# Half of the residual row carried by each of a token's two expert results, in a top-2 mixture-of-experts block

## The chip, the cores and the metric

The kernel runs on one core of a Trainium2 chip. The metric is the device time of one execution in microseconds (us), median of several runs. Five engines work beside each other and meet only through semaphores: TensorE (PE), VectorE (DVE), ScalarE (ACT), GpSimd (POOL) and SyncE (SP), which here only issues DMAs.

## The reference, cut to what matters

One sequence of 2048 tokens of 128 numbers in float32 goes through one layer: gated linear attention, a layer norm, a feed-forward stage of 8 experts of which each token uses its best 2, and a second layer norm.

```python
x = _layernorm(x + attn(x))                    # no scale and no shift in the norm
# expert stage
scores = x @ Wr + br
weights = softmax(scores of the best 2 of 8)   # 0 elsewhere
for i in range(E):
    h = relu(x @ W1[i] + b1[i])
    out += (h @ W2[i] + b2[i]) * weights[i]
return _layernorm(x + out)
```

The row `x` added in the last line is the residual row that the change is about.

## The kernel before, in words

Tokens are held in T = 16 tiles of 128: token 128 t + p lies in partition p of tile t. The program has four stages.

1. Projections (first 59 us). `x_sb` [128, 16, 128] is loaded and transposed by PE; q, k, v, the gates and the decay factors are made by PE, ACT and DVE. Meanwhile SP issues the DMAs that fill the DRAM buffer `expert_rows` with padding rows (L389), then those of the second expert weights and biases (L391, L393). GpSimd makes constants, scales the first group of keys (`scale_k(0)`), and then waits for all padding rows (`pool.wait_ge(s_pad, 16 * E)`, L493), since it is to scatter real rows over them.
2. Attention and routing (59 to 145.6 us), a software pipeline over the 16 tiles. DVE's `residual(t)` (L886) adds `x_sb` to the attention output in PSUM, `mean_var` and ACT's `inverse_std` (L643, L647) give the norm's factors, and `normalize` (L925) writes the normalized row to `xr[:, t, 0, 0:D]`; ACT copies it to `xr[:, t, 1, 0:D]`, and its transpose to `x1T` (L633) for the router matmul. GpSimd scatters each token's row twice (once for each expert, with the weight in column D and the number of the result row in column D + 1) into `expert_rows` by indirect DMA (L489).
3. Experts (145.6 to 247.5 us). 39 slots of 128 rows, each of one expert. For each slot SP gathers the rows to `xg` (L407) and 2 of 3 slots' first weights; PE transposes the rows (L1321), ACT copies the transpose to `xgT` (L688), PE makes the hidden layer (L1333) and the output (L1346), ACT and DVE apply bias and relu (L698, L1066), DVE adds the bias `b2` (L1074) and multiplies by the token's weight (`weighted`, L1079, into `yw`). GpSimd takes the result row numbers (L529, `dest`) and scatters the 128 rows of `yw` to `expert_results` by indirect DMA (L533). Every third slot's first weights are loaded from GpSimd's queue (L373).
4. The last stage (247.5 to 266.0 us). A token's two results lie next to each other in `expert_results`. SP loads them in 8 groups of FT = 2 tiles (L417, `ysum`). For each group GpSimd adds the first result to the residual row in `xr` (L546), DVE adds the second result (L1100), takes `bn_stats` and `bn_aggr` of both tiles (L1103, L1106), ACT makes 1/sqrt(var + eps) with a Ln and an Exp (L714, L716), DVE makes the shift -mean/std (`shift`, L1095, one group behind), ACT applies scale and shift to each tile (L721), and SP stores the group (L421).

Each engine's order is its program order as written; nothing is scheduled otherwise. The functions that the diff touches:

Of the kernel before, what the change touches and what calls it, by code (L numbers as in the profile page):

```python
# [24 lines left out]
def build(nc, x, Wq, Wk, Wv, Wg, Wgk1, Wgk2, bgk2, Wo, g_norm, Wr, br, W1, b1, W2, b2, out):  # L25
# [23 lines left out]
    out_tok = out.rearrange("a (t p) d -> p (a t) d", p=P)  # L49
    rows = nc.dram_tensor("expert_rows", [E * CAP, ROW], F32, kind="Internal").ap()  # L50
    results = nc.dram_tensor("expert_results", [TOP * N, D], F32, kind="Internal").ap()

    with ExitStack() as ctx:
        def sb(name, shape, dt=F32):
            return ctx.enter_context(nc.sbuf_tensor(name, shape, dt))
# [126 lines left out]
        fshift = sb("fshift", [P, T])  # L182
# [21 lines left out]
        s_w2 = sem("w2_loaded")  # L204
        s_seed = sem("constants_zeroed")
# [82 lines left out]
        s_acc0 = sem("first_result_added")  # L288
        s_acc = sem("second_result_added")
# [4 lines left out]
        s_fshift = sem("final_shift")  # L294
# [83 lines left out]
        def _(sp):  # L378
# [37 lines left out]
            for g in range(T // FT):  # L416
                sp.dma_start(ysum[:, g * FT:(g + 1) * FT, :],  # L417
                             results[g * FT * P * TOP:(g + 1) * FT * P * TOP, :].rearrange("(t p k) d -> p t (k d)", p=P, k=TOP)).then_inc(s_ysum[g], 16)
            for g in range(T // FT):
                sp.wait_ge(s_result, (g + 1) * FT)  # L420
                sp.dma_start(out_tok[:, g * FT:(g + 1) * FT, :], result[:, g * FT:(g + 1) * FT, :]).then_inc(s_stored, 16)  # L421
# [3 lines left out]
        def _(pool):  # L425
# [38 lines left out]
            count_up(xr[:, :, :, ROW - 1], [[TOP * P, T], [1, TOP]], 0, TOP)  # L464
            def scale_k(g):
                c = slice(g * GROUP, (g + 1) * GROUP)
                t = slice(g * TG, (g + 1) * TG)
                pool.wait_ge(s_eq, 2 * (g + 1))
                pool.tensor_tensor(km[:, c], kT[:, c], ek[:, g % 2, :], ALU.mult).then_inc(s_km, 1)  # L469
                pool.wait_ge(s_km, g + 1)  # L470
                pool.tensor_tensor(tiles(kc[:, c]), tiles(km[:, c]), wide(er[:, t], P), ALU.mult).then_inc(s_kc, 1)
# [71 lines left out]
            for g in range(T // FT):  # L543
                t = slice(g * FT, (g + 1) * FT)
                pool.wait_ge(s_ysum[g], 16)
                pool.tensor_tensor(acc[:, t, :], ysum[:, t, 0:D], xr[:, t, 0, 0:D], ALU.add).then_inc(s_acc0, 1)  # L546

        @block.scalar
        def _(act):
# [80 lines left out]
            def copy_x1T(t):  # L630
                if t >= 2:
                    act.wait_ge(s_dve_bank, t - 2 + AGE_ROUTE)
                act.activation(x1T[:, t % 2, :], bank[6][:, P:2 * P], ACT.Copy).then_inc(s_x1T, 1)  # L633
# [5 lines left out]
            def inverse_std(t):  # L639
# [3 lines left out]
                act.activation(lstd[:, b, :], mv[:, b, 1:2], ACT.Ln, bias=eps_sb[:, :]).then_inc(s_lstd, 1)  # L643
# [39 lines left out]
            def copy_rows(i):  # L683
                h = i % 3
                act.wait_ge(s_gt, i + 1)
                if i >= 3:
                    act.wait_ge(s_hb, i - 2)
                act.activation(xgT[:, h, :], bank[7][:, 0:P], ACT.Copy).then_inc(s_gT, 1)  # L688
# [21 lines left out]
            for g in range(T // FT + 1):  # L710
                if g < T // FT:
                    t = slice(g * FT, (g + 1) * FT)
                    act.wait_ge(s_fmv, (g + 1) * FT)
                    act.activation(flog[:, t], fmv[:, t, 1], ACT.Ln, bias=eps_sb[:, :]).then_inc(s_flog, 1)  # L714
                    act.wait_ge(s_flog, g + 1)
                    act.activation(frstd[:, t], flog[:, t], ACT.Exp, scale=-0.5).then_inc(s_frs, 1)  # L716
                if g:
                    act.wait_ge(s_frs, g)
                    act.wait_ge(s_fshift, g)
                    for n in range((g - 1) * FT, g * FT):  # L720
                        act.activation(result[:, n, :], acc[:, n, :], ACT.Identity, bias=fshift[:, n:n + 1],  # L721
                                       scale=frstd[:, n:n + 1]).then_inc(s_result, 1)

        @block.vector
        def _(dve):
# [94 lines left out]
            dve.tensor_scalar(wo_sb[:, :, :], wo_in[:, :, :], gnorm_sb[:, 0:1], None, ALU.mult).then_inc(s_wo2, 1)  # L820
# [64 lines left out]
            def residual(t):  # L885
                dve.tensor_tensor(res[:, t % 2, :], bank[7][:, 256:256 + D], x_sb[:, t, :], ALU.add).then_inc(s_res, 1)  # L886
# [182 lines left out]
            def weighted(i):  # L1069
# [9 lines left out]
                dve.tensor_scalar(yw[:, u, :], yb[:, h, :], xg[:, u, D:D + 1], None, ALU.mult).then_inc(s_yw, 1)  # L1079
# [11 lines left out]
            def shift(g):  # L1091

                t = slice(g * FT, (g + 1) * FT)
                dve.wait_ge(s_frs, g + 1)
                dve.scalar_tensor_tensor(fshift[:, t], fmv[:, t, 0], -1.0, frstd[:, t], ALU.mult, ALU.mult).then_inc(s_fshift, 1)  # L1095

            for g in range(T // FT):
                t = slice(g * FT, (g + 1) * FT)
                dve.wait_ge(s_acc0, g + 1)
                dve.tensor_tensor(acc[:, t, :], acc[:, t, :], ysum[:, t, D:2 * D], ALU.add).then_inc(s_acc, 1)  # L1100
                dve.wait_ge(s_acc, g + 1)
# [5 lines left out]
                if g:  # L1107
                    shift(g - 1)
            shift(T // FT - 1)
# [277 lines left out]
```

## Time and profile before

| | |
|---|---|
| median of 3 runs | 265.79 us (264.65, 265.79, 267.12) |
| span of the profiled execution | 266.0 us, 0.2 us above the median |
| busy: PE, DVE, POOL, ACT | 185.6, 159.6, 119.0, 110.9 us |
| stage borders used here | 59, 145.6, 247.5, 266.0 us |

The profiled execution is listed by its span alone, from the first to the last instruction; no other time of that execution is shown. Times in the profile are microseconds from the span's start. A timeline row holds the start, the duration, the engine, the line of the kernel, the operation with its output and inputs, and how many instructions are merged in it. "[4.01 <-DMA ...]" says how long the engine had sat idle before, and what ended that. SPq and POOLq are the queues that issue DMAs. Where a row merges several instructions, its duration is that of the whole run of them.

### The profile page before, as it was taken

What the parts mean: (1) busy time and instruction counts of PE and PEld (TensorE: products, weight loads), DVE (VectorE), ACT (ScalarE), POOL (GpSimd) and SP (SyncE); (2) the same over time, 40 slices, a digit from 0 to 9 for tenths busy, and PEclk for the clock granted to TensorE, in tenths of its full rate; (3) what the DMA queues carried; (4) which work ended last, traced back from release to release, by engine and by line L of the source; (5) the groups of instructions that cost most, each with busy time, mean ns of one, the idle gap of its engine ahead of it and who ended that gap; (6) DMA issues with size and microseconds to landing.
All of it is one profiled execution on the core that took longest, in us unless ns stands there. A gap on an engine that the chain in (4) does not pass through costs nothing.

```text
span 266.0 us, 5740 instructions
## 1 busy us (share of the span) xinstructions
PE 185.6 (70%) x1289; PEld 150.2 (56%) x1289; DVE 159.6 (60%) x593; ACT 110.9 (42%) x345; POOL 119.0 (45%) x188
## 2 busy tenths in 40 slices
PE   2999959205886898896652188999889998994000
PEld 1556427104654676664541178989889898893000
DVE  5399937005989988878676022555555556563293
ACT  1188764201645355454530022444434434440086
POOL 5000400014522746556576614566666666666270
PEclk9999995955999799999855557999999999999555
DMA  5999999998000010010011445466666575630563
GB/s 166 254 187 194 199 174 183 188 196 264 0 2 1 10 34 24 27 34 30 30 41 50 110 150 159 135 194 192 192 184 185 184 182 177 175 108 1 178 198 99
DMA packets 39553, 33.87 MB, mean 127 GB/s; under 512 B 3806, under 2 KB 33172, under 8 KB 39520
## 3 DMA queue, kind: packets, MB, share of 16 engines
q1 hardware_dynamic: 35264, 25.68, 45.5%
q0 software_dynamic: 3312, 7.64, 8.1%
q10 hardware_dynamic: 944, 0.17, 0.3%
q8 instruction: 12, 0.20, 0.3%
q14 instruction: 21, 0.17, 0.2%
HBM read 19.15 MB, written 14.79 MB: 128 GB/s over the span
## 4 chain that ended last, share of the span: by engine, by line
issue 49%; SPq 24%; POOL 12%; PE 4%; DVE 3%; DMA 3%; POOLq 2%; ACT 2%; DVEq 0%; ACTq 0%
SPq L389 15%; POOL expert_results L533 8%; SPq L393 4%; POOL dest L529 2%; PE psum L1333 2%; SPq L391 2%; ACT x_sb L721 1%; PE psum L1346 1%; POOLq L363 1%; DMA gate<-expert_results 1%; DVE fstats L1103 1%; DMA expert_results<-kT,dest 1%; DMA xg<-expert_rows 1%; SPq L380 1%; DVE xT L1100 1%
## 5 line engine op out<-in xcount | busy, mean ns | idle before, releaser
L533 POOL DMA_INDIRECT expert_results<-kT,dest x39 | 38.4, 985 | 36.3 <-issue 18.2
L1346 PE MATMUL psum<-w_sb,gT 128*128 x312 | 44.0, 286 | 0.5 <-issue 0.3
L1066 DVE TENSOR_SCALAR gT<-psum,b_sb 128x128 f32<-128x128 f32 x78 | 23.8, 347 | 32.3 <-PE psum L1333 19.1
L1346 PEld LDWEIGHTS psum<-w_sb,gT 128*128 128x128 f32 x312 | 39.4, 198 | 2.2 <-issue 1.3
L489 POOL DMA_INDIRECT expert_rows<-xr,slot x32 | 31.4, 980 | 13.1 <-issue 10.8
L698 ACT ACTIVATE gT<-psum,b_sb 128x128 f32<-128x128 f32 x78 | 24.4, 363 | 18.2 <-issue 15.5
L688 ACT ACTIVATE kT<-psum 128x128 f32<-128x128 f32 x39 | 10.8, 277 | 46.0 <-PE psum L1321 37.0
L469 POOL TENSOR_TENSOR km<-kT,ek 128x512 f32<-128x512 f32 x4 | 5.1, 1279 | 50.7 <-DMA expert_rows<-pad_row 25.9
L1333 PE MATMUL psum<-kT,km 128*128 128x128 f32 x168 | 24.2, 292 | 5.1 <-issue 5.1
L1333 PEld LDWEIGHTS psum<-kT,km 128*128 128x128 f32 x168 | 22.0, 205 | 6.1 <-issue 6.1
L479 POOL TENSOR_TENSOR rgate<-rrms,gate 128x256 f32<-128x256 f32 x16 | 12.0, 752 | 27.7 <-ACT rrms L625 26.7
L1235 PE MATMUL psum<-wo_sb,ogT 128*128 128x128 f32 x64 | 11.8, 316 | 15.5 <-DVE ogT L919 15.5
L1333 PE MATMUL psum<-kT,qm 128*128 128x128 f32 x144 | 20.2, 286 | 1.6 <-issue 1.6
L1074 DVE TENSOR_TENSOR kT<-psum,b_sb 128x128 f32<-128x128 f32 x39 | 11.4, 292 | 16.0 <-issue 9.6
L1235 PEld LDWEIGHTS psum<-wo_sb,ogT 128*128 128x128 f32 x64 | 11.0, 222 | 16.8 <-DVE ogT L919 14.5
L1333 PEld LDWEIGHTS psum<-kT,qm 128*128 128x128 f32 x144 | 18.3, 200 | 2.2 <-issue 2.2
L900 DVE SCALAR_TENSOR_TENSOR state<-state,tile_decay,psum 32x64 f32<-32x64 f32 x60 | 16.3, 272 | 2.3 <-PE psum L1230 0.7
L620 ACT ACTIVATE lrms<-psum,eps_sb 128x256 f32<-128x256 f32 x16 | 7.5, 471 | 23.6 <-PE psum L1226 17.8
L919 DVE TENSOR_TENSOR ogT<-psum,rgate 128x256 f32<-128x256 f32 x16 | 6.8, 423 | 15.8 <-POOL rgate L479 15.4
L1321 PE MATMUL psum<-ident,xg 128*128 128x128 f32 x39 | 11.3, 290 | 6.8 <-DMA xg<-expert_rows 6.8
L1221 PE MATMUL psum<-sq,block_ones 128*128 128x256 f32 x32 | 11.9, 455 | 3.5 <-ACT sq L651 2.8
L882 DVE COPY_PREDICATED aT<-keep,psum 128x512 f32<-128x512 int32 x16 | 11.6, 724 | 4.0 <-PE psum L1195 3.9
(169 smaller groups left out, 382.6 us busy)
## 6 DMA issues: line engine op xcount, KB each, us to landing
expert_rows<-pad_row SPq DMA_DIRECT2D x8, 1105.0 KB, 18.8
km<-in_L_ffn_W_dram SPq DMA_DIRECT2D x14, 256.0 KB
qm<-in_L_ffn_W_dram SPq DMA_DIRECT2D x12, 256.0 KB
xg<-expert_rows SPq DMA_DIRECT2D x39, 65.0 KB
gate<-expert_results SPq DMA_DIRECT2D x8, 256.0 KB, 4.6
km<-in_L_ffn_W_dram POOLq DMA_DIRECT2D x7, 256.0 KB
qm<-in_L_ffn_W_dram POOLq DMA_DIRECT2D x6, 256.0 KB
x_sb<-in_L_attn_x_dram SPq DMA_DIRECT2D x4, 256.0 KB, 4.3
```

Source lines behind the costliest of these rows:

```text
L389: sp.dma_start(rows[e * CAP:(e + 1) * CAP, :].rearrange("(n p) c -> p n c", p=P), pad_row[:, :].unsqueeze(1).to_broadcast([P, CAP // P, RO ...
L479: pool.tensor_tensor(rgate[:, t % 2, :, :], rrms[:, t % 2, :, :], gate[:, :, t * P:(t + 1) * P], ALU.mult).then_inc(s_rg, 1)
L489: pool.indirect_dma_start(out=rows[:, :], in_=xr[:, t, k, :], in_offset=None, out_offset=bass.IndirectOffsetOnAxis(ap=slot[:, t, k:k + 1], ...
L533: pool.indirect_dma_start(out=results[:, :], in_=yw[:, u, :], in_offset=None, bounds_check=TOP * N - 1, oob_is_err=False, out_offset=bass. ...
L698: act.activation(hT[:, h, n, :], bank[2 * (i % 2)][:, n * P:(n + 1) * P], ACT.Relu, bias=b1_sb[:, bass.ds(e * HC + n, 1)]).then_inc(s_hTa, 1)
L882: dve.copy_predicated(aT[:, t % 2, :, :], keep[:, :].unsqueeze(1).to_broadcast([P, HEADS, P]), psum[:, 0:HEADS, 0:P]).then_inc(s_aT, 1)
L900: ins = dve.scalar_tensor_tensor(state[r, t % 2, v], state[r, (t - 1) % 2, v], tile_decay[r, t:t + 1], bank[7][r, v], ALU.mult, ALU.add)
L1066: dve.tensor_scalar(hT[:, h, HC // 2 + n, :], bank[2 * (i % 2) + 1][:, n * P:(n + 1) * P], b1_sb[:, bass.ds(e * HC + HC // 2 + n, 1)], 0.0 ...
L1221: return mm(bank[6][:, 256:512], block_ones[:, :], sq[:, t % 2, :, :].rearrange("p c t -> p (c t)"), start=True, stop=True)
L1235: last = mm(bank[7][:, 256:256 + D], ogT[:, t % 2, c, :], wo_sb[:, c, :], start=(c == 0), stop=(c == DVC - 1))
L1333: last = mm(bank[2 * (i % 2) + half][:, k * P:(k + 1) * P], w1_buf[u][:, n * P:(n + 1) * P], xgT[:, h, :], start=True, stop=True)
L1346: last = mm(bank[4 + i % 2][:, 0:D], hT[:, h, n, :], w2_all[:, bass.ds(first + n * D, D)], start=(n == 0), stop=(n == HC - 1))
```

## The change: what it does

- GpSimd multiplies all of `x_sb` by 0.5 once, after the last transpose of it, and the projection `Wo` is multiplied by 0.5 besides its norm weight. So the sum of residual and attention is half of what it was; `inverse_std` multiplies the variance by 4, and the normalized row in `xr` comes out at half its value. The router's and the experts' inputs are doubled back in the copies that ACT makes anyway (`scale=2.0`).
- In the expert stage DVE's last step of a slot becomes `scalar_tensor_tensor`: bias output times weight, plus the gathered (half) row. A token's two results then sum to residual plus expert output.
- In the last stage partition p holds tokens 16 p to 16 p + 15, so a group of 2 tokens is one piece of 2 KB per partition in DRAM when loaded (before: 2 pieces of 1 KB) and 1 KB when stored (before: 2 of 512 B). The two results are added by DVE in the even groups and by GpSimd in the odd ones. GpSimd, no longer ACT, applies mean and 1/std, with `tensor_scalar` on each 128x128 tile; the shift step is gone.

```diff
-    out_tok = out.rearrange("a (t p) d -> p (a t) d", p=P)
+    out_rows = out.rearrange("a (p j) d -> p (a j) d", p=P)
+    results_tok = results.rearrange("(p j k) d -> p j (k d)", p=P, k=TOP)
@@ SP, last stage
-                sp.dma_start(ysum[:, g * FT:(g + 1) * FT, :],
-                             results[g * FT * P * TOP:(g + 1) * FT * P * TOP, :].rearrange("(t p k) d -> p t (k d)", p=P, k=TOP)).then_inc(s_ysum[g], 16)
+                sp.dma_start(ysum[:, g * FT:(g + 1) * FT, :], results_tok[:, g * FT:(g + 1) * FT, :]).then_inc(s_ysum[g], 16)
-                sp.dma_start(out_tok[:, g * FT:(g + 1) * FT, :], result[:, g * FT:(g + 1) * FT, :]).then_inc(s_stored, 16)
+                sp.dma_start(out_rows[:, g * FT:(g + 1) * FT, :], result[:, g * FT:(g + 1) * FT, :]).then_inc(s_stored, 16)
@@ GpSimd, before scale_k(0)
+            pool.wait_ge(s_job, at["xT", NG - 1] + 1)
+            pool.tensor_scalar(x_sb[:, :, :], x_sb[:, :, :], 0.5, None, ALU.mult).then_inc(s_xhalf, 1)
@@ GpSimd, last stage
             for g in range(T // FT):
-                t = slice(g * FT, (g + 1) * FT)
-                pool.wait_ge(s_ysum[g], 16)
-                pool.tensor_tensor(acc[:, t, :], ysum[:, t, 0:D], xr[:, t, 0, 0:D], ALU.add).then_inc(s_acc0, 1)
+                if g % 2 == 0:
+                    t = slice((g + 1) * FT, (g + 2) * FT)
+                    pool.wait_ge(s_ysum[g + 1], 16)
+                    pool.tensor_tensor(acc[:, t, :], ysum[:, t, 0:D], ysum[:, t, D:2 * D], ALU.add).then_inc(s_acc_odd, 1)
+                pool.wait_ge(s_frs, g + 1)
+                for n in range(g * FT, (g + 1) * FT):
+                    pool.tensor_scalar(result[:, n, :], acc[:, n, :], fmv[:, n, 0:1], frstd[:, n:n + 1],
+                                       ALU.subtract, ALU.mult).then_inc(s_result, 1)
@@ ACT
-                act.activation(x1T[:, t % 2, :], bank[6][:, P:2 * P], ACT.Copy).then_inc(s_x1T, 1)
+                act.activation(x1T[:, t % 2, :], bank[6][:, P:2 * P], ACT.Copy, scale=2.0).then_inc(s_x1T, 1)
-                act.activation(lstd[:, b, :], mv[:, b, 1:2], ACT.Ln, bias=eps_sb[:, :]).then_inc(s_lstd, 1)
+                act.activation(lstd[:, b, :], mv[:, b, 1:2], ACT.Ln, bias=eps_sb[:, :], scale=4.0).then_inc(s_lstd, 1)
-                act.activation(xgT[:, h, :], bank[7][:, 0:P], ACT.Copy).then_inc(s_gT, 1)
+                act.activation(xgT[:, h, :], bank[7][:, 0:P], ACT.Copy, scale=2.0).then_inc(s_gT, 1)
@@ ACT, last stage: Ln and Exp stay, the scaling goes
-                if g:
-                    act.wait_ge(s_frs, g)
-                    act.wait_ge(s_fshift, g)
-                    for n in range((g - 1) * FT, g * FT):
-                        act.activation(result[:, n, :], acc[:, n, :], ACT.Identity, bias=fshift[:, n:n + 1],
-                                       scale=frstd[:, n:n + 1]).then_inc(s_result, 1)
@@ DVE
-            dve.tensor_scalar(wo_sb[:, :, :], wo_in[:, :, :], gnorm_sb[:, 0:1], None, ALU.mult).then_inc(s_wo2, 1)
+            dve.tensor_scalar(wo_sb[:, :, :], wo_in[:, :, :], gnorm_sb[:, 0:1], 0.5, ALU.mult, ALU.mult).then_inc(s_wo2, 1)
             def residual(t):
+                if t == 0:
+                    dve.wait_ge(s_xhalf, 1)
-                dve.tensor_scalar(yw[:, u, :], yb[:, h, :], xg[:, u, D:D + 1], None, ALU.mult).then_inc(s_yw, 1)
+                dve.scalar_tensor_tensor(yw[:, u, :], yb[:, h, :], xg[:, u, D:D + 1], xg[:, u, 0:D],
+                                         ALU.mult, ALU.add).then_inc(s_yw, 1)
@@ DVE, last stage (the calls of shift(g) go too)
-                dve.wait_ge(s_acc0, g + 1)
-                dve.tensor_tensor(acc[:, t, :], acc[:, t, :], ysum[:, t, D:2 * D], ALU.add).then_inc(s_acc, 1)
-                dve.wait_ge(s_acc, g + 1)
+                if g % 2:
+                    dve.wait_ge(s_acc_odd, g // 2 + 1)
+                else:
+                    dve.wait_ge(s_ysum[g], 16)
+                    dve.tensor_tensor(acc[:, t, :], ysum[:, t, 0:D], ysum[:, t, D:2 * D], ALU.add).then_inc(s_acc, 1)
+                    dve.wait_ge(s_acc, g // 2 + 1)
```

## Rows read from the trace of the kernel before

**Rows 1.** The stretches of the four stages: busy time by engine, granted clock, DMA.

```profile
0.00:59.00 59.00, 39.99 (x159) 23.79 (x159) 32.69 (x77) 27.35 (x50) 6.34 (x27) 0.89 1.16 192
59.00:145.60 86.60, 62.24 (x467) 46.89 (x467) 68.77 (x312) 38.34 (x146) 47.45 (x56) 0.85 0.14 44
145.60:247.50 101.90, 83.36 (x663) 79.51 (x663) 47.90 (x156) 35.17 (x117) 58.62 (x97) 0.92 0.53 153
247.50:266.00 18.50, 0.00 (x0) 0.00 (x0) 10.29 (x48) 10.07 (x32) 6.57 (x8) 0.50 0.55 171
```

**Rows 2.** The chain that ended last: its shares of the span by line.

```profile
SPq L389 15%; POOL expert_results L533 8%; SPq L393 4%; POOL dest L529 2%; PE psum L1333 2%; SPq L391 2%; ACT x_sb L721 1%; PE psum L1346 1%; POOLq L363 1%; DMA gate<-expert_results 1%; DVE fstats L1103 1%; DMA expert_results<-kT,dest 1%; DMA xg<-expert_rows 1%; SPq L380 1%; DVE xT L1100 1%
```

**Rows 3.** Timeline around the padding wait, 48 to 62 us.

```profile
48.90 0.26 ACT L628 ACTIVATE kcT<-psum 128x128 f32<-128x128 f32 x1
...
59.01 1.26 POOL L469 TENSOR_TENSOR km<-kT,ek 128x512 f32<-128x512 f32 x1 [25.91 <-DMA expert_rows<-pad_row]
...
62.10 0.42 DVE L919 TENSOR_TENSOR ogT<-psum,rgate 128x256 f32<-128x256 f32 x1 [15.05 <-POOL rgate L479]
```

**Rows 4.** Timeline of the projections: PE's last transpose, then DVE.

```profile
12.03 0.60 PE L1126 MATMUL psum<-ident,x_sb 128*128 128x128 f32 x4
...
15.17 0.68 DVE L771 SCALAR_TENSOR_TENSOR gT<-km,qm 128x512 f32<-128x512 f32 x1
```

**Rows 5.** Timeline of the expert stage's end, 242 to 247 us.

```profile
242.80 0.29 DVE L1079 TENSOR_SCALAR kT<-kT,xg 128x128 f32<-128x128 f32 x1
243.32 0.98 POOL L533 DMA_INDIRECT expert_results<-kT,dest  x1 [0.78 <-DVE kT L1079]
...
245.27 0.97 POOL L533 DMA_INDIRECT expert_results<-kT,dest  x1 [0.78 <-POOL dest L529]
```

**Rows 6.** Timeline of the last stage: loads, the first group, ACT's final run.

```profile
247.48 4.16 SPq L417 DMA_DIRECT2D gate<-expert_results  x8
250.26 1.76 POOL L546 TENSOR_TENSOR xT<-gate,xr 128x256 f32<-128x256 f32 x2 [4.01 <-DMA gate<-expert_results]
...
251.47 0.49 DVE L1103 BATCH_NORM_STATS2 fstats<-xT 128x6 f32<-128x128 f32 x2
251.87 0.30 DVE L1106 BATCH_NORM_AGGREGATE fmv<-fstats 128x2 f32<-128x6 f32 x2
...
252.21 0.30 ACT L714 ACTIVATE flog<-fmv,eps_sb 128x2 f32<-128x2 f32 x1 [11.81 <-DVE fmv L1106]
...
252.54 0.20 ACT L716 ACTIVATE frstd<-flog 128x2 f32<-128x2 f32 x1
...
262.08 1.63 ACT L721 ACTIVATE x_sb<-xT,fshift,frstd 128x128 f32<-128x128 f32 x4
```

**Rows 7.** GpSimd's groups by shape: count, busy us, mean ns, idle before.

```profile
L529 POOL CAST dest<-xg 128x1 uint32<-128x1 f32 x39 | 7.8, 200 | 0.1
...
L469 POOL TENSOR_TENSOR km<-kT,ek 128x512 f32<-128x512 f32 x4 | 5.1, 1279 | 50.7 <-DMA expert_rows<-pad_row 25.9 <-ACT ek L592 24.8
...
L444 POOL TENSOR_SCALAR_AFFINE_SELECT causal<-causal 128x128 f32<-128x128 f32 x1 | 0.3, 292 | 0.1
```

**Rows 8.** The 8 GpSimd additions of the last stage: ns min/median/max.

```profile
L546 POOL TENSOR_TENSOR xT<-gate,xr x8: 714/824/973, 250.3 to 256.9; 128x256 f32<-128x256 f32 x8
```

**Rows 9.** DVE's shift beside GpSimd's additions, and after them.

```profile
254.72 0.63 DVE L1095 SCALAR_TENSOR_TENSOR fshift<-fmv,frstd 128x2 f32<-128x2 f32 x1
...
259.07 0.13 DVE L1095 SCALAR_TENSOR_TENSOR fshift<-fmv,frstd 128x2 f32<-128x2 f32 x1
```

**Rows 10.** Engines, clock, DMA share and GB/s while the results are being loaded.

```profile
250.26:256.00 5.74, 0.00 (x0) 0.00 (x0) 4.83 (x20) 2.87 (x10) 4.69 (x6) 0.50 0.93 302
```

**Rows 11.** The stores' DMA issues: KB each, median us to landing.

```profile
out_dram<-x_sb SPq DMA_DIRECT2D x8, 128.0 KB, 1.8
```

**Rows 12.** DVE's two groups that price the expert step's new form.

```profile
L1100 DVE TENSOR_TENSOR xT<-xT,gate 128x256 f32<-128x256 f32 x8 | 3.3, 415 | 7.9 <-POOL xT L546 7.9
...
L771 DVE SCALAR_TENSOR_TENSOR gT<-km,qm 128x512 f32<-128x512 f32 x4 | 2.7, 682 | 0.0
```

More of the change, by code:

```diff
@@ L181, in build @@
         frstd = sb("frstd", [P, T])
-        fshift = sb("fshift", [P, T])
         result = x_sb
@@ L204, in build @@
         s_w2 = sem("w2_loaded")
+        s_xhalf = sem("x_halved")
         s_seed = sem("constants_zeroed")
@@ L287, in build @@
         s_ysum = [sem(f"results_loaded{g}") for g in range(T // FT)]
-        s_acc0 = sem("first_result_added")
-        s_acc = sem("second_result_added")
+        s_acc = sem("even_results_added")
+        s_acc_odd = sem("odd_results_added")
         s_fst = sem("final_stats")
@@ L293, in build @@
         s_frs = sem("final_rstd")
-        s_fshift = sem("final_shift")
         s_result = sem("result_done")
@@ L709, in _ @@
                 act_step(i)
[L710 to L716, printed above, removed]
-                if g:
-                    act.wait_ge(s_frs, g)
-                    act.wait_ge(s_fshift, g)
-                    for n in range((g - 1) * FT, g * FT):
-                        act.activation(result[:, n, :], acc[:, n, :], ACT.Identity, bias=fshift[:, n:n + 1],
-                                       scale=frstd[:, n:n + 1]).then_inc(s_result, 1)
+            for g in range(T // FT):
+                t = slice(g * FT, (g + 1) * FT)
+                act.wait_ge(s_fmv, (g + 1) * FT)
+                act.activation(flog[:, t], fmv[:, t, 1], ACT.Ln, bias=eps_sb[:, :]).then_inc(s_flog, 1)
+                act.wait_ge(s_flog, g + 1)
+                act.activation(frstd[:, t], flog[:, t], ACT.Exp, scale=-0.5).then_inc(s_frs, 1)
         @block.vector
@@ L1089, in _ @@
                 dve_step(i)
[L1091 to L1095, printed above, removed]
             for g in range(T // FT):
                 t = slice(g * FT, (g + 1) * FT)
-                dve.wait_ge(s_acc0, g + 1)
-                dve.tensor_tensor(acc[:, t, :], acc[:, t, :], ysum[:, t, D:2 * D], ALU.add).then_inc(s_acc, 1)
-                dve.wait_ge(s_acc, g + 1)
+                if g % 2:
[4 more added lines that the diff above has]
+                    dve.wait_ge(s_acc, g // 2 + 1)
                 for n in range(g * FT, (g + 1) * FT):
@@ L1106, in _ @@
                     dve.bn_aggr(fmv[:, n, :], fstats[:, n, :]).then_inc(s_fmv, 1)
-                if g:
-                    shift(g - 1)
-            shift(T // FT - 1)
         @block.tensor
```

## The prediction, made before the changed kernel had run

> **What bounds the kernel now.** I read the profile in the order of the program's stages, since its engines are busy in different ones. The windows by stage [rows 1] show that no engine fills any stage by itself: 59 us of projections, 86.6 of attention, 101.9 of experts, 18.5 of the last stage. So for each stage I asked what ends last.
>
> In the projections it is the padding: its issues on SP's queue are the largest named share of the chain of waits, 15% [rows 2], and the timeline shows the engines stopped: ACT's last work is at 48.90, GpSimd has sat idle 25.91 us until the padding rows landed at 59.01, and DVE goes on at 62.10 after 15.05 us of idle time [rows 3]. Whatever is finished by about 49 us could be finished ten later.
>
> In the attention stage the change only alters operands of steps that are there anyway.
>
> In the experts it is GpSimd's scatters. The chain of waits names L533 and L529 with 8 and 2% [rows 2]; at the stage's end the last result row block is ready at 242.80 + 0.29 = 243.09, but its scatter starts at 245.27, behind the one of 243.32 [rows 5]. The distance of two scatters, 1.95 us, is GpSimd's own, and DVE is 2.2 us ahead of it.
>
> In the last stage the loads are issued from 247.48, the first group is there at 250.26, and ACT's last scaling ends at 262.08 + 1.63 = 263.71 [rows 6]; 2.3 us of store and end follow. Of the 13.45 us in between, the first part goes at DVE's pace, and there is a wait in it: the tiny shift takes 0.63 us beside GpSimd's additions and 0.13 us after them [rows 9]. So the change is worth something only in these 18.5 us, and costs something wherever it lengthens a chain that ends last.
>
> **The change part by part.** *Halving `x_sb`, on GpSimd.* It starts when PE's last transpose is over, 12.03 + 0.60 = 12.63 [rows 4]. GpSimd's fixed cost is 0.20 us (a one-column cast), its slope for one input (292 - 200)/128 = 0.72 ns a column, by the 512-column product with two inputs (1279 - 200)/512 = 2.11 ns [rows 7]. For 2048 columns that is 1.7 to 4.5 us, so it ends between 14.3 and 17.1. It may hold up DVE's two-input steps from 15.17 on [rows 4] by at most 2 us; `scale_k(0)` behind it on GpSimd comes at 30 us, and the DVE wait for it at 64 us. All of this lies before the padding wait with its ten idle microseconds [rows 3]: zero. If that cover were gone it would cost up to 2 us. `Wo` with a second factor, and the factors 2 and 4 in ACT's copies and Ln, are the same instructions with another constant: zero.
>
> *The expert step.* One DVE instruction in 39 slots changes from `tensor_scalar` (0.29 us [rows 5]) to a two-input form. From 128x512 at 682 ns and 128x256 at 415 ns [rows 12] I get 1.04 ns a column, so 415 - 133 = 282 ns for 128 columns: the same. Bounds: 0 to 0.1 us a slot, and DVE has 2.2 us before GpSimd takes the row block [rows 5]. GpSimd's queue is untouched. I take zero; once, at the stage's start where DVE is on the chain, it could be 0.1.
>
> *The last stage, rebuilt.* The program order gives this loop for a pair of groups, even e and odd o. GpSimd adds o; DVE takes its statistics; ACT does Ln and Exp; GpSimd meanwhile scales e, then scales o when the Exp is there, and only then adds the next odd group. The return trip from the start of an addition to the odd group's factors: addition 0.73 (the undisturbed ones, 714 ns [rows 8]), hand-over 0.03, statistics of both tiles from 251.47 to 252.17 = 0.70, hand-over 0.04, Ln and Exp from 252.21 to 252.74 = 0.53 [rows 6], hand-over to GpSimd 0.10. Sum 2.13. Then two scalings of length s and 0.05 to the next addition: one pair takes 2.18 + 2s, as long as the even group's two scalings fit in the 1.40 us between the end of the addition and the factors. DVE's work for a pair (0.42 + 2 x 0.70, 0.42 from [rows 12]) is 1.8 and hides.
>
> The length s of a 128x128 `tensor_scalar` on GpSimd is not in the trace. From below: the fixed cost alone, 0.20; a one-input select of that size, 0.29; by the two-input slope, 200 + 128 x 2.11 = 0.47 [rows 7]. From above: the addition of twice the columns with two inputs, 0.73 to 0.82 [rows 8]. I take 0.38, between the select and the slope, since it has one input tensor but two column operands.
>
> The first odd group lands one group after the first: while the loads run, 302 GB/s are moved [rows 10], so 262 KB take 0.87 us, 250.26 + 0.87 = 251.1. Four pairs: 251.1 + 4 x (2.18 + 2s) - 0.05 = 259.8 + 8s. With s = 0.38 the last result is there at 262.8, against 263.7: -0.9. With 0.29: -1.6; with 0.20: -2.3; with 0.47: -0.2; it breaks even at 0.49. The loads end near 256 us and the fourth pair starts at 259.9, so they only bound the first pair.
>
> *The layout.* Loads in pieces of 2 KB in place of 1 KB, stores in 1 KB in place of 512 B. The DMA share is 0.93 in the load window [rows 10], so the engines are full there and larger pieces can bring the first landings forward: 0 to 0.6 us of the 3.6 between first issue and first odd group; strided reads could cost 0.3 instead. I take -0.3. The last store lands in 1.8 us [rows 11]: -0.3 to +0.1, taken at -0.1.
>
> The Trainium skill (DMA: Bandwidth & Descriptors, "Why small descriptors are slow") says that each packet carries a fixed overhead of a few bus cycles; an estimate by that page, some 3 in 35 for a 1 KB piece against 3 in 67, would be 4% of the load time, near the low end of that bound. No row here has 2 KB results to compare.
>
> *The lock.* The shift waiting for GpSimd [rows 9] shows that a DVE instruction with two SBUF inputs and a GpSimd instruction exclude each other. In the new loop only DVE's addition of the even group is such a step, 0.42 us. It asks at 1.46 us into the pair, when the scalings of e (0.76 to 1.52 at s = 0.38) are ending, and GpSimd then waits for the factors anyway: zero at this s, 0.4 a pair, 1.6 in all, if s is over about 0.6. The Trainium skill (SBUF — State Buffer, "Who interferes with whom") states this as an exclusive lock held for the whole instruction; by that rule, the trace agrees (0.63 beside, 0.13 after).
>
> **Sum.** -0.9 - 0.3 - 0.1 = -1.3 us against the profiled 266.0, whose span stands 0.2 above the median; applied to the median of 265.79 it gives 264.5.
>
> **The rivals.** *A: the scaling on GpSimd is dear (slower).* If a `tensor_scalar` with two column operands costs as much as the addition of 256 columns, s = 0.75, the even group's scalings (1.50) outlast the return trip (1.40), GpSimd is the bound, and a pair is 0.73 + 4s + 0.08 = 3.81. The last result comes at 251.1 + 15.2 = 266.3, 2.6 later; with the layout's -0.4 that is 268.0 us. It loses from s = 0.49 on (0.54 with the layout's gain), and by 16s instead of 8s from 0.70. For it: no GpSimd row has this form, and its two-input product is twice as slow as DVE's, 1279 against 682 ns [rows 7, 12]. Against it: the select of the same size at 0.29 [rows 7]. The Trainium skill (GPSIMD Engine Reference, "Engine selection") advises against elementwise work there, about 2 times slower for two inputs, roughly line rate for one; no run so far shows the one-input case with arithmetic.
>
> *B: everything cheap.* s near 0.22, since GpSimd overlaps instructions that don't wait for each other, and loads 0.6, store 0.3 earlier: 259.8 + 1.8 - 0.6 = 261.0, -2.7 - 0.3 = -3.0: 262.8 us. For it: DMA share 0.93 while loading. Against it: the return trip doesn't shrink.
>
> *C: the cover fails.* The halving pushes DVE's projections, and the padding is not what ends them; or the new expert step reaches GpSimd's chain, 39 x 0.1 = 3.9. With -1.3 that gives 266 to 268.5 us. Against it: ten and 2.2 us of slack.
>
> *D: no gain to speak of.* GpSimd takes over ACT's role with the same length, s = 0.49 and the layout worth nothing: 265.8.
>
> **How the numbers follow.** 1% is 2.7 us (263.1 to 268.4), about what a measurement of this kernel can tell from no change. The forecast with D (s from 0.28 to 0.54, 263.3 to 266) has 0.63, B 0.20, A 0.12, C 0.05. B lies on the border of 1%, and the steps I may have missed there would take it further, so all its 0.20 counts as faster; of A and C some 0.10 is slower by over 1%, 0.07 within. That gives 0.20, 0.70, 0.10. The range goes from B's 262.8 to 267.3 (A at s = 0.7), with about 0.1 left out on each side.
>
> **What would show it.** In the changed profile: the padding wait on GpSimd still ends at 59 with the same start of DVE after it; scatters at the end of the experts still 1.95 us apart; in the last stage GpSimd's additions 2.9 us apart with an idle gap of about 0.6 us before each odd group's scaling, ended by ACT's Exp; a `tensor_scalar` of 0.3 to 0.45 us; first load landed by 250.3 or earlier relative to its issue. Wrong would make it: GpSimd without a gap (A), a gap ended by a load (the layout reads slower), or a changed border at 145.6 or 247.5.

## The result, and the profile after

The changed kernel takes 273.92 us (median of 4 runs, 271.94 to 277.83) against 265.80: the ratio is 1.032, 95% interval 1.023 to 1.041. It is 8 us slower where 1.3 us less was forecast. Medians here are over all runs; ratios and intervals leave out the runs that were over 1.5% above a kernel's fastest, and the profiles of e3, e8 and e10 are of such runs.

The profiled execution has a span of 271.7 us and a time of its own of 273.35. So 1.6 us lie outside the span, as in every later run of the layer that lists both.

I went through the stages in the order of [rows 1]. The first is the timeline at the two waits that the prediction relied on (start, duration, engine, line, operation):

```profile
14.94 5.40 POOL L465 TENSOR_SCALAR x_sb<-x_sb 128x2048 f32<-128x2048 f32 x1 [9.46 <-PE psum L1123]
...
17.30 1.86 DVE L771 SCALAR_TENSOR_TENSOR gT<-km,qm 128x512 f32<-128x512 f32 x1
19.19 1.22 DVE L776 TENSOR_TENSOR_SCAN cum<-seg,gT 128x512 f32<-128x512 f32 x1
...
54.08 1.26 POOL L471 TENSOR_TENSOR km<-kT,ek 128x512 f32<-128x512 f32 x1 [17.68 <-DMA expert_rows<-pad_row]
```

The halving takes 5.40 us, more than the bound of 4.5, and the two-input step that DVE starts beside it takes 1.86 us (0.68 before), until 19.16. The halving itself ends at 20.34, 1.2 us later, and DVE's next two-input step, at 19.19, takes 1.22 us as before the change. Behind the halving GpSimd still waits 17.68 us for the padding, so the cover of [rows 3] holds. That the padding is there 4.9 us earlier than before is not the change's doing: the same program, profiled on another chip (a0 below), has it at 59.47, and the other eleven profiles of this layer have it between 58.4 and 60.2.

Now the last stage, where the rows answer to [rows 6]:

```profile
245.13 3.84 SPq L417 DMA_DIRECT2D gate<-expert_results  x8
247.87 0.42 DVE L1100 TENSOR_TENSOR xT<-gate 128x256 f32<-128x256 f32 x1 [7.05 <-DMA gate<-expert_results]
...
252.81 0.71 POOL L549 TENSOR_TENSOR xT<-gate 128x256 f32<-128x256 f32 x1
253.52 3.27 POOL L552 TENSOR_SCALAR x_sb<-xT,fmv,frstd 128x128 f32<-128x128 f32 x4
253.56 0.49 DVE L1103 BATCH_NORM_STATS2 fstats<-xT 128x6 f32<-128x128 f32 x2 [2.40 <-POOL xT L549]
...
256.76 0.72 POOL L549 TENSOR_TENSOR xT<-gate 128x256 f32<-128x256 f32 x1
...
261.41 3.11 POOL L552 TENSOR_SCALAR x_sb<-xT,fmv,frstd 128x128 f32<-128x128 f32 x4
```

GpSimd's scalings follow its addition without a gap, four in 3.27 us, and the next addition comes 256.76 - 252.81 = 3.95 us after the last one. DVE sits idle for 2.4 us a pair. The line's own statistics (ns min/median/max), and the windows (busy us of PE, PEld, DVE, ACT, POOL with counts; clock; DMA share; GB/s), say the same: GpSimd is busy for all of 10.5 us.

```profile
L552 POOL TENSOR_SCALAR x_sb<-xT,fmv,frstd x16: 782/789/947, 249.7 to 263.7; 128x128 f32<-128x128 f32 x16
```

```profile
254.00:264.50 10.50, 0.00 (x0) 0.00 (x0) 3.69 (x21) 2.50 (x10) 10.50 (x14) 0.50 0.21 70
264.50:266.50 2.00, 0.00 (x0) 0.00 (x0) 0.00 (x0) 0.00 (x0) 0.02 (x1) 0.50 0.19 66
266.50:271.70 5.20, 0.00 (x0) 0.00 (x0) 0.00 (x0) 0.00 (x0) 0.00 (x0) 0.50 0.00 0
```

The last two windows were the surprise. The final store has landed at 266.5, no engine is busy, nothing is moved, and the span goes on for 5.2 us. The waits of SP's queue put a name to it, first after, then before:

```profile
SPq L54 <- PEq L54: 5.0, 1, 5.0
```

```profile
SPq L53 <- PEq L53: 0.2, 1, 0.2
```

Line 54 is the line at which the program's block closes, and every engine waits there for every other. The name PEq is not the cause: PE had been through its closing DRAIN, the last instruction that each engine has before this common wait, at 240. I listed the sequencers' own records from the trace, which the views leave out since they are not busy time:

```
start     us    engine  instruction                (changed kernel)
262.76  8.71    GpSimd  DRAIN                       line 54
263.73  0.79    GpSimd  TENSOR_SCALAR               line 552, the last one
264.55  0.33    Sync    DMA_DIRECT2D                line 420, the last store
266.50  0.04    Sync    COMPARE_BRANCH              line 54, the store has landed
271.52  0.02    GpSimd  EVENT_SEMAPHORE             line 54
                                                    (kernel before)
256.52  8.31    GpSimd  DRAIN                       line 53
256.91  0.97    GpSimd  TENSOR_TENSOR               line 546, the last one
265.57  0.04    Sync    COMPARE_BRANCH              line 53, the store has landed
265.79  0.02    GpSimd  EVENT_SEMAPHORE             line 53
```

GpSimd's closing DRAIN ends 6.96 us after its last instruction in both: 264.52 to 271.48 after, 257.88 to 264.84 before, where it was 0.7 us ahead of the last store's landing (265.57). In the old last stage nobody waited for it, by those 0.7 us.

The last stage, from the first load issue, then reads ("last result" is the start of the last store's issue, 0.03 us after the last scaling has ended):

| | before | after | |
|---|---|---|---|
| first load issue to last result | 16.26 | 19.42 | +3.2 |
| last result to the end | 2.25 | 7.17 | +4.9 |
| last stage | 18.5 | 26.6 | +8.1 |

The rest of the program ended 2.35 us earlier in this profile (247.48, 245.13). I put that down to scatter and not to the change; the first experiment after this shows how much of it there is.

### The profile page after: what moved, and what is told of

Read it like the earlier page. It is cut to its first block, busy times and chain, and to the rows that moved or that the text cites. A ratio compares the mean times of both kernels' runs of the same rounds, so it can differ in the third digit from the quotient of the medians.

```text
span 271.7 us, 5718 instructions
## 1 busy us (share of the span) xinstructions
PE 188.0 (69%) x1289; PEld 151.9 (56%) x1289; DVE 160.8 (59%) x581; ACT 105.2 (39%) x329; POOL 134.0 (49%) x201
## 4 chain that ended last, share of the span: by engine, by line
issue 36%; PE 30%; SPq 22%; POOL 6%; DMA 3%; DVE 1%; POOLq 0%; ACT 0%; DVEq 0%
PE psum L1330 14%; PE psum L1343 14%; SPq L389 13%; POOL x_sb L552 4%; SPq L393 4%; SPq L391 2%; PE psum L1318 2%; DMA gate<-expert_results 1%; DMA xg<-expert_rows 1%; DMA expert_results<-kT,dest 1%; POOL xT L549 1%; SPq L380 1%; SPq L385 0%; SPq L398 0%; SPq L401 0%
## 5 line engine op out<-in xcount | busy, mean ns | idle before, releaser
L1343 PEld LDWEIGHTS psum<-w_sb,gT 128*128 128x128 f32 x312 | 38.7, 195 | 1.6 <-issue 0.4
L1330 PE MATMUL psum<-kT,qm 128*128 128x128 f32 x144 | 19.4, 278 | 2.3 <-issue 2.3
L1330 PEld LDWEIGHTS psum<-kT,qm 128*128 128x128 f32 x144 | 17.5, 192 | 3.1 <-issue 3.1
L1232 PE MATMUL psum<-wo_sb,ogT 128*128 128x128 f32 x64 | 12.7, 333 | 7.4 <-DVE ogT L921 7.4
L1232 PEld LDWEIGHTS psum<-wo_sb,ogT 128*128 128x128 f32 x64 | 11.8, 238 | 8.9 <-DVE ogT L921 6.4
L1081 DVE SCALAR_TENSOR_TENSOR kT<-kT,xg 128x128 f32<-128x128 f32 x39 | 13.8, 353 | 1.4
```

Source lines behind the costliest of these rows:

```text
L1081: dve.scalar_tensor_tensor(yw[:, u, :], yb[:, h, :], xg[:, u, D:D + 1], xg[:, u, 0:D], ALU.mult, ALU.add).then_inc(s_yw, 1)
L1232: last = mm(bank[7][:, 256:256 + D], ogT[:, t % 2, c, :], wo_sb[:, c, :], start=(c == 0), stop=(c == DVC - 1))
L1330: last = mm(bank[2 * (i % 2) + half][:, k * P:(k + 1) * P], w1_buf[u][:, n * P:(n + 1) * P], xgT[:, h, :], start=True, stop=True)
L1343: last = mm(bank[4 + i % 2][:, 0:D], hT[:, h, n, :], w2_all[:, bass.ds(first + n * D, D)], start=(n == 0), stop=(n == HC - 1))
```

## The experiments

The two chips on which these ran are slower with the kernel before as well (medians 271.06 to 271.37), so each ratio is against the runs of before on its own chip, and single stages are compared within profiles.

Theory 1: the loss is GpSimd's dear scaling plus its closing DRAIN. Theory 2: other parts of the change (halving, expert step, layout) carry it, or the DRAIN is tied to what GpSimd did just before.

**a0_changed_again.** The changed kernel, no edit, on another chip. 

> The changed kernel itself, on the chip of the next three. Both theories: 2.5 to 4% over the kernel before on this chip; closing DRAIN 6.96 us after GpSimd's last scaling, 19.4 us from the first load issue to the last result.

Median 278.3 (4 runs) against 271.06 (13 runs), 1.027; no interval was given. By the runs that a ratio counts (275.11 and 277.0 against seven of 267.37 to 271.06) it is about 1.02, at the lower edge of what was expected. Load to last result 19.59, DRAIN 6.96, tail 7.17: the last stage is the same to 0.2 us. The middle is not: from the padding to the first gather it took 88.65 us here and 92.57 in the first profile, and 88.80 in the kernel before. The windows of the two executions of one kernel, this one and then the first, show where:

```profile
59.50:148.00 88.50, 63.08 (x467) 47.33 (x467) 69.16 (x312) 38.33 (x146) 48.02 (x57) 0.85 0.14 43
```

```profile
54.00:146.60 92.60, 65.24 (x467) 49.60 (x467) 70.87 (x312) 38.67 (x146) 49.07 (x58) 0.82 0.13 41
```

The same 467 matmuls are busy 2.2 us longer at a mean granted clock of 0.82 against 0.85. So 4 us of scatter in one stage come without any change, and a stage's length is only worth comparing where several profiles agree. Over the thirteen profiles of this layer the stretch takes 87.6 to 94.2 us, with short and long ones in both kernels.

**e1_act_scales.** The scaling goes back to ACT, all else stays changed:

```diff
@@ GpSimd, last stage
-                pool.wait_ge(s_frs, g + 1)
-                for n in range(g * FT, (g + 1) * FT):
-                    pool.tensor_scalar(result[:, n, :], acc[:, n, :], fmv[:, n, 0:1], frstd[:, n:n + 1],
-                                       ALU.subtract, ALU.mult).then_inc(s_result, 1)
@@ ACT and DVE, last stage: as in the kernel before
+                    act.wait_ge(s_fshift, g)
+                    for n in range((g - 1) * FT, g * FT):
+                        act.activation(result[:, n, :], acc[:, n, :], ACT.Identity, bias=fshift[:, n:n + 1],
+                                       scale=frstd[:, n:n + 1]).then_inc(s_result, 1)
+                if g:
+                    shift(g - 1)
```

> The changed kernel, but ACT applies shift and 1/std as before the change; GpSimd keeps the odd additions. Theory 1 (GpSimd's scaling of 0.79 us a tile, and the 6.95 us that GpSimd's closing DRAIN takes after its last instruction, are the whole loss): the last addition ends near 8.5 us after the first load issue, the DRAIN ends before or with the last store, and the time falls to 263 to 265 us. Theory 2 (halving, the new expert step or slower middle stages carry the loss): it stays at 268 us or above.

Ratio to before 0.987 (0.974 to 0.999). The expected 263 to 265 us were reckoned from 265.8; from this chip's 271.2 they are 268.4 to 270.4, and 268.1 was measured. Load to last result 15.10, tail 2.35: 17.45 in all, 9.1 less than the changed kernel and 1.1 less than before. By the ratio the whole time is 3.6 us under before (interval 0.2 to 7); the last stage accounts for 1.1 of it, and the rest is not explained. The last addition ends 9.60 us after the first load issue, not the 8.5 expected, so GpSimd's DRAIN (over at 264.87) is only 0.5 us ahead of the last store's landing. Halving, expert step and layout are all still in it. Theory 2's first half falls.

**e2_drain_probe.** The kernel before, plus

```diff
+            pool.wait_ge(s_result, T)
+            pool.memset(pair_slot[:, :], 0.0)
```

> The kernel before, with one memset of 128x1 on GpSimd after the last result is there, nothing else. Theory 1 (the closing DRAIN of GpSimd takes a fixed 6.95 us after its last instruction): memset at about 263.9, DRAIN to 271, end 5 us later than before: 270.5 to 271.5 us. Theory 2 (the DRAIN's length belongs to what GpSimd did before, or to the tensor_scalar instructions of the changed kernel): within 0.7 us of before, 266.5 at most.

Ratio 1.024 (1.015 to 1.033), 5.7 us by the medians. One memset of one column puts 5 us on the end (tail 7.31, 2.25 before). It stands in the timeline,

```profile
267.21 0.10 POOL L548 MEMSET pair_slot<- 128x1 f32 x1 [5.96 <-ACT x_sb L723]
```

and the wait of SP's queue at the block's end grows from 0.2 to

```profile
SPq L53 <- PEq L53: 5.2, 1, 5.2
```

Memset over at 267.32, DRAIN over at 274.26: 6.94. So the length does not belong to the scaling: a memset is enough, and what matters is when it ends.

**e3_front_alone.** The kernel before, plus the 128x2048 multiplication, by 1.0:

```diff
+            pool.wait_ge(s_job, at["xT", NG - 1] + 1)
+            pool.tensor_scalar(x_sb[:, :, :], x_sb[:, :, :], 1.0, None, ALU.mult).then_inc(s_xhalf, 1)
@@ DVE, residual(t)
+                if t == 0:
+                    dve.wait_ge(s_xhalf, 1)
```

> The kernel before, with the 128x2048 multiplication of x_sb on GpSimd (by 1.0) and DVE's wait for it, nothing else. Theory 1: 5.4 us on GpSimd that hold DVE up by about 1.2 us in the projections and are covered by the padding wait: 0, within 1 us of before. Theory 2 (the front is not covered; the attention stage gets the loss): 2 to 5 us slower.

Ratio 0.999 (0.992 to 1.006). The front costs nothing that can be measured, though DVE's step beside it took 1.87 us here too. The last stage, where this kernel is the kernel before, took 17.16 us to the last result. In the four profiles with that code (before, e2, e3, e9) it is 16.26, 16.43, 17.16 and 16.49: the scatter of this stage can be 0.9 us.

**e4_immediates.** The changed kernel, with constants in place of the column operands (it leaves out the last normalization):

```diff
-                    pool.tensor_scalar(result[:, n, :], acc[:, n, :], fmv[:, n, 0:1], frstd[:, n:n + 1],
+                    pool.tensor_scalar(result[:, n, :], acc[:, n, :], 0.5, 2.0,
```

> The changed kernel, but GpSimd scales with the constants 0.5 and 2.0 in place of the two column operands; it leaves out the normalization of the last stage. If the column operands are what makes the instruction dear: from the halving's 5.40 us for 2048 columns, 2.54 ns a column, 0.5 us a tile; a pair 3.2 to 3.3 us in place of 3.9, and 2.5 to 2.8 us faster than the changed kernel, 271.3. If the two operations or the instruction's fixed part cost it: 0.79 us a tile and 273.9.

```profile
L552 POOL TENSOR_SCALAR x_sb<-xT x16: 638/642/723, 255.4 to 267.3; 128x128 f32<-128x128 f32 x16
```

0.64 us a tile, not the 0.5 expected of constants nor the 0.79 of the rival. Load to last result 17.41 in place of 19.5, so 2.1 us less; the tail stays at 7.18, and the ratio to before is 1.022 (1.012 to 1.032). Cheaper scaling alone doesn't help enough: 4.9 of the 8.1 us are the DRAIN. Why 0.64, e9 shows.

**e5_gpsimd_idle.** e1 with all additions on DVE, so GpSimd ends with its last scatter:

```diff
-                pool.tensor_tensor(acc[:, t, :], ysum[:, t, 0:D], ysum[:, t, D:2 * D], ALU.add).then_inc(s_acc_odd, 1)
@@ DVE: every group
+                dve.wait_ge(s_ysum[g], 16)
+                dve.tensor_tensor(acc[:, t, :], ysum[:, t, 0:D], ysum[:, t, D:2 * D], ALU.add).then_inc(s_acc, 1)
```

> The changed kernel with ACT's scaling (as in e1_act_scales) and all additions of the last stage on DVE, so GpSimd has nothing after its last scatter. Theory 1 (DRAIN has a fixed length, whatever came before): the DRAIN ends 6.96 us after the last scatter instruction, long before the end, and counts for nothing. DVE has 8 x 1.25 = 10 us of work, ACT 9.5: 15 to 16 us from load to last result, total within 1 us of e1_act_scales, 1 to 1.5% under before. Rival (the DRAIN waits for outstanding indirect DMAs or for the block's end): its length differs clearly from 6.96 us after a scatter.

Ratio 0.989 (0.982 to 0.997); 14.44 to the last result, under the 15 to 16 expected, and tail 2.34. The DRAIN ends at 251.77, 6.94 us after the last scatter (244.83) and 11 us before the end: the length is the same after an indirect DMA. ACT is now what ends last, 1.19 us a group, while DVE is through:

```profile
257.64 0.30 DVE L1111 BATCH_NORM_AGGREGATE fmv<-fstats 128x2 f32<-128x6 f32 x2
...
258.85 1.63 ACT L720 ACTIVATE x_sb<-xT,fshift,frstd 128x128 f32<-128x128 f32 x4
```

**e5b_gpsimd_idle.** The same kernel with more rounds. 

> e5_gpsimd_idle again, with more rounds: 14.4 us from load to last result and a tail of 2.3, so 1.7 us less than the kernel before in the last stage, and 0.5 to 1.1% under it in the times.

Ratio 0.995 (0.989 to 1.000); 14.66 and 2.34 us. The last stage repeats to 0.2 us here; the whole is faster than before by 0.5 and 1% in the two sets of runs, with intervals that reach from 1.8% to nothing.

**e7_old_layout.** e1 with the old mapping of tokens to partitions, in the stores (shown) and in the loads:

```diff
-    out_rows = out.rearrange("a (p j) d -> p (a j) d", p=P)
+    out_tok = out.rearrange("a (t p) d -> p (a t) d", p=P)
```

> e1_act_scales with the old layout of the last stage (token 128 t + p in partition p; loads in 1 KB and stores in 512 B pieces). If the layout is worth the 0.4 us that the prediction gave it: 15.5 us from load to last result, tail 2.3 to 2.4. If the larger pieces are worth more: 16 us and above. If strided reads cost: below 15.1.

Ratio 0.988 (0.981 to 0.995), as e1. 14.46 us to the last result, tail 3.19: 17.65 against e1's 17.45. The tail has a term that I had not looked for. GpSimd's additions each wait for a load,

```profile
259.93 0.72 POOL L552 TENSOR_TENSOR xT<-gate 128x256 f32<-128x256 f32 x1 [1.36 <-DMA gate<-expert_results]
```

and SP's queue waits at the block's end again:

```profile
SPq L54 <- PEq L54: 1.1, 1, 1.1
```

The last addition ends 10.45 us after the first load issue (9.60 in e1), and 6.96 us later is 1.1 us after the last store has landed.

Read alone, the pair says two things: the larger pieces bring the last load in 0.85 us sooner, and, by the branch that was written down, strided reads cost 0.6 us at the last result (15.10 against 14.46). The other traces bear out neither. By their records of when each load had landed, the last of the eight was there 9.01 to 9.66 us after the first issue in the five profiles with 1 KB pieces (before, e2, e3, e7, e9; median 9.37), and 8.80 to 9.63 us in the eight with 2 KB pieces (median 9.24); e7 and e1 lie at opposite ends. And most of e1's 0.6 us is one meeting of DVE's addition with GpSimd's (DVE's and GpSimd's rows of e1):

```profile
255.94 0.76 POOL L551 TENSOR_TENSOR xT<-gate 128x256 f32<-128x256 f32 x1 [0.61 <-DMA gate<-expert_results]
```

```profile
256.02 0.96 DVE L1111 TENSOR_TENSOR xT<-gate 128x256 f32<-128x256 f32 x1
```

DVE's other three additions there, and all four in e7, take 0.42 to 0.43 us. So the layout is worth nothing that can be seen, at the last load or at the last result.

**e8_split_scaling.** Meant to beat both kernels; e1 with GpSimd adding groups 1 and 3 alone, and

```diff
@@ DVE, in shift(g)
+                if g >= T // FT - 2:
+                    n = (g + 1) * FT - 1
+                    dve.tensor_scalar(result[:, n, :], acc[:, n, :], fmv[:, n, 0:1], frstd[:, n:n + 1],
+                                      ALU.subtract, ALU.mult).then_inc(s_result_dve, 1)
```

> A version meant to beat both: e1_act_scales, GpSimd adds only groups 1 and 3 (so its DRAIN ends early), and DVE scales the second tile of the last two groups. Theory 1: ACT loses 0.86 us at the end, DVE has room for it: 14.3 us from load to last result, 0.8 us under e1_act_scales, 1.5% under before. If the end is set elsewhere (loads, stores): as e1_act_scales.

Ratio 0.992 (0.983 to 1.001); 14.75 and 2.49 us. The 0.8 us over e1 did not show in the times; in the stage it is 0.2 (17.24 against 17.45).

**e10_idle_and_split.** e5 with DVE's two tiles of e8. 

> e5_gpsimd_idle, with the second tile of the last two groups scaled by DVE. ACT ended that kernel at 1.19 us a group with DVE idle for the last 2.5 us: 13.5 us from load to last result, 0.9 us under e5b_gpsimd_idle, about 1% or more under before. If the loads or stores set the end instead: as e5b.

Ratio 0.988 (0.976 to 1.000); 13.88 us to the last result, 0.6 and 0.8 under e5's two profiles where 0.9 was expected, and a tail of 2.49, which gives 0.15 of it back. The last stage is 16.4 us, 2.1 us under before and the shortest of all; in the whole time it can't be told from e5 or e1.

**e9_forms_on_gpsimd.** The disputed instruction by itself. The kernel before, and after its last result, 3 times 7 instructions on GpSimd, each waiting for the one ahead:

```diff
+                        ins = pool.tensor_scalar(b, a, 0.5, None, ALU.mult)
+                        ins = pool.tensor_scalar(b, a, 0.5, 2.0, ALU.subtract, ALU.mult)
+                        ins = pool.tensor_scalar(b, a, frstd[:, 0:1], None, ALU.mult)
+                        ins = pool.tensor_scalar(b, a, fmv[:, 0, 0:1], frstd[:, 0:1], ALU.subtract, ALU.mult)
+                        ins = pool.tensor_tensor(b, a, qc[:, D:2 * D], ALU.add)
+                        ins = pool.tensor_copy(b, a)
+                        ins = pool.tensor_scalar(kc[:, 0:4 * D], qc[:, 0:4 * D], 0.5, None, ALU.mult)
```

> The kernel before, with 21 instructions on GpSimd after the last result, each waiting for the one ahead: three times tensor_scalar of 128x128 with one constant, with two constants, with one column, with two columns, tensor_tensor of 128x128, a copy of 128x128, and tensor_scalar of 128x512 with one constant; DVE and ACT are idle. From e4_immediates (0.64) and the changed kernel (0.79): two constants 0.64, two columns 0.79. If each operation costs: one constant 0.5 and one column 0.55 to 0.6. If a pass of either form costs the same: 0.64 and 0.7. By the halving's slope of 2.54 ns a column: 1.5 us for 512 columns, and 0.5 for 128. The closing DRAIN again 6.96 us after the last of them.

Groups by line (shapes, count, busy us, mean ns, idle before), in the order of their cost:

```profile
L566 POOL TENSOR_SCALAR kc<-qc 128x512 f32<-128x512 f32 x3 | 4.5, 1497 | 0.3
L560 POOL TENSOR_SCALAR kc<-qc,fmv,frstd 128x128 f32<-128x128 f32 x3 | 2.4, 805 | 0.3
L556 POOL TENSOR_SCALAR kc<-qc 128x128 f32<-128x128 f32 x3 | 2.0, 654 | 0.2
L558 POOL TENSOR_SCALAR kc<-qc,frstd 128x128 f32<-128x128 f32 x3 | 1.8, 607 | 0.3
L554 POOL TENSOR_SCALAR kc<-qc 128x128 f32<-128x128 f32 x3 | 1.6, 538 | 6.1 <-ACT x_sb L744 5.9
L562 POOL TENSOR_TENSOR kc<-qc 128x128 f32<-128x128 f32 x3 | 1.4, 453 | 0.3
L564 POOL COPY kc<-qc 128x128 f32<-128x128 f32 x3 | 0.9, 293 | 0.2
```

One constant costs 0.54, a second operation 0.12 more, a column in place of a constant 0.07 to 0.08 each: 0.54 + 0.12 + 0.15 = 0.81. From 128 to 512 columns it is (1497 - 538) / 384 = 2.5 ns a column, the same slope as the halving's 5.40 us, and steeper than that of the two-input product (2.1 by [rows 7]). A copy of this size costs what the select did, 0.29. Each carries a wait, and they come out a little above the same forms back to back: 805 against 789 ns in the changed kernel, 654 against 642 in e4.

**e11_no_gpsimd_dma.** A kernel that leaves out the layer: SP loads x, GpSimd does 8 `tensor_scalar`, SP stores.

```diff
+            for n in range(8):
+                pool.tensor_scalar(x_sb[:, n, :], x_sb[:, n, :], 0.5, None, ALU.mult).then_inc(s_half, 1)
```

> What the closing DRAIN of GpSimd belongs to. A kernel that leaves out the whole layer: SP loads x, GpSimd does 8 tensor_scalar of 128x128, SP stores x; GpSimd issues no DMA. If the 6.95 us are there in every kernel: DRAIN ends 6.95 us after the last tensor_scalar. If they belong to a GpSimd queue that has issued DMAs (the kernel's very first DRAIN, ahead of all of them, took 0.19 us): under 0.5 us. Its time says nothing of the layer.

```profile
6.91 4.00 POOL L69 TENSOR_SCALAR x_sb<-x_sb 128x128 f32<-128x128 f32 x8 [6.48 <-DMA x_sb<-in_L_attn_x_dram]
```

```
 6.88  4.09    GpSimd  DRAIN            line 51
10.37  0.53    GpSimd  TENSOR_SCALAR    line 69, the last one
```

The last instruction ends at 10.90, the DRAIN at 10.97: 0.07 us. So the 6.95 us are not the price of every closing. All thirteen profiles that have them are of programs in which GpSimd's queue has issued DMAs, and this one has none; but this one also lacks everything else of the layer, so that the DMAs bring them is likely and not shown. Whether it would be the direct ones (L373) or the indirect ones (L489, L533), and what is waited for in that time, was not tried.

## Why the prediction was wrong

*What bounds each stage*: right for projections, attention and experts. The scatters at the experts' end are still 1.95 us apart in the changed kernel (240.98, 242.93). For the last stage it was incomplete: the prediction wrote "2.3 us of store and end follow" and took that as a constant. Three things end there, the last store, the closing of each engine, and with it GpSimd's DRAIN, and I costed the move of work to GpSimd without asking what follows GpSimd's last instruction. **This is the step that failed: the constant tail should have been the later of two ends, that of the last store and GpSimd's last instruction plus 6.96.** It is worth +4.9 us of the 8.1, e2 shows it with a memset alone, and no rival had it. The row that shows it was not in any busy view: DRAIN is a sequencer's instruction.

*The length s of a scaling*: 0.38 taken, 0.79 measured. That is inside what the prediction had read from above (0.73 to 0.82) and a little over rival A's 0.75. It is the second term that failed, worth +3.2 us where -0.9 was forecast. The loop itself was built right: with s over 0.70, "GpSimd is the bound, and a pair is 0.73 + 4s + 0.08", which for 0.79 gives 3.97, and 3.95 was measured. The term was mis-sized because a select and a cast stood for "one input"; a `tensor_scalar` costs 2.5 ns a column with a single input, more than the two-input product. Rival A (268.0) had this mechanism, its price (+2.6, measured +3.2) and its bound; what it lacks to 273.9 is the DRAIN's 4.9, 0.6 in the scaling and the 0.4 that it took off for the layout. The page that I cited beside it (the Trainium skill, GPSIMD Engine Reference, "Engine selection") calls one-input work there roughly line rate. The trace disagrees for `tensor_scalar`: 128 columns at 538 ns and 512 at 1497, against 427 ns for DVE's two-operation one of 512 columns (its group by line L790 in the trace before).

*The layout*, taken at -0.4: nothing. The first odd group, to which -0.3 was given, landed 3.44 to 3.56 us after the first issue in the old layout and 3.35 to 3.95 in the new one; the last load is no different either (under e7); and the last store took 1.8 us from its issue to the end of the wait for it before and 1.95 after, where -0.1 was taken. An estimate by the Trainium skill (DMA: Bandwidth & Descriptors, "Why small descriptors are slow") was 4% of the load time. That would be 0.4 us of 9.4; equal layouts differ by more than that here, so no run shows it or rules it out.

*The lock*: seen where it was not forecast to matter. DVE's 0.68 us step beside the halving took 1.86. But in all three profiles (this one, a0, e3) it was through 1.2 us before the halving was, so a lock held for the whole instruction, as the prediction has it, is not what these rows show. In the last stage of the changed kernel DVE's addition of the even group took 0.39 to 0.48 us beside GpSimd's scalings, and two of GpSimd's scalings stretched from 0.79 to 0.95; this is 0.3 us in all, where the prediction gave 1.6 for s over 0.6. Where both engines add, it weighs more: DVE's 128x256 addition, 0.39 to 0.43 us by itself, took 0.93 to 0.98 once each in e1, e2 and e9 and twice in e3, and at no time in the profile of before. Part of the last stage's scatter is this.

*Halving and expert step*, both at zero: e3 says 0.999 for the halving, and e1, which has both, is no slower than before; the expert step was not tried by itself. The expert step's mean went from 326 to 353 ns, within its bound of 0.1 us.

*The base of the sum*: I set the span of 266.0 beside the median of 265.79 and called it 0.2 above. With the 1.6 us that lie outside every span, the profiled execution of before was nearer to 267.6, and its median 1.8 below. The difference forecast is not touched by it. Nor is it by a slip in the range for D: by the prediction's own sum s = 0.28 gives 263.7, not 263.3.

## What to carry to other kernels

Before moving work to another engine at the end of a program, ask what that engine still has to do after its last instruction: in this layer GpSimd's last instruction should end 7 us before the last store lands, and whether that holds in another program its closing DRAIN's record tells. Price an elementwise step on GpSimd by its own form (operation, number of operations, column operands), not by its element count; for this shape every form of `tensor_scalar` was dearer there than an addition of two tensors. And when a window shows no engine busy and no data moving, list the sequencers' records before believing the engine that the wait is put down to.

## What the runs showed of the hardware that I had not expected

- GpSimd's closing DRAIN ends 6.94 to 6.96 us after its last instruction in twelve profiles of this layer, after an addition, a scaling, a memset or a scatter; 0.07 us in a small program without DMAs from its queue (and without the rest of the layer). In e9, where its last step was a wait, it took 6.93 us from its own start.
- `tensor_scalar` 128x128 on GpSimd: 538 ns with a constant, 654 with two, 607 with a column, 805 with two columns; copy 293, `tensor_tensor` 453.
- The same program on the same data spent 88.7 and 92.6 us in its attention stage, with mean granted clocks of 0.85 and 0.82.
- Eight loads of 256 KB were all in 9.01 to 9.66 us after the first issue in pieces of 1 KB (five profiles), and 8.80 to 9.63 us in pieces of 2 KB (eight).
- A DVE addition of 128x256 took 0.39 to 0.43 us by itself and 0.93 to 0.98 where it met one of GpSimd's.
